# New keys of all eight heads weighed in one passage at a batch's end, with two heads' outputs in each PSUM bank

## What is computed

```python
q = rope(rmsnorm(x @ Wq.T))          # 32 query heads of 128
k = rope(rmsnorm(x @ Wk.T))          # 8 key heads of 128, 32 new keys per sequence
v = x @ Wv.T
k_all = concat([k_cache[block_table], k])    # 512 cached keys, then 32 new ones
v_all = concat([v_cache[block_table], v])
scores = einsum('bqhd,bkhd->bhqk', q, repeat(k_all)) * SCALE      # 4 query heads share a key head
probs = softmax(where(valid, scores, -1e30))
o = einsum('bhqk,bkhd->bqhd', probs, repeat(v_all))
return x + einsum('bse,de->bsd', o.reshape(b, s, 4096), Wo)
```

## Time and profile before

| | us |
|---|---|
| median of 3 runs | 2317.36 |
| lowest and highest | 2316.82, 2319.02 |
| the profiled execution | 2317.06 |
| its span, first to last instruction | 2315.2 |
| TensorE busy in the span | 2260.6 |
| VectorE busy | 1701.7 |
| ScalarE busy | 1296.3 |
| GpSimd busy | 1148.0 |
| attention's weighing, first to last instruction | 732.5 to 1950.3 |

### The profile page before, as it was taken

One profiled execution on the slowest core, in us unless ns is written; L12 is line 12 of the kernel. 1 busy time (PEld: TensorE's weight loads), 2 busy tenths in 40 slices (PEclk: granted clock), 3 DMA queues, 4 the chain that ended last, 5 costly groups with the idle time before them and its releaser, 6 DMA issues. The chain is left out here.

```text
span 2315.2 us, 52251 instructions
## 1 busy us (share of the span) xinstructions
PE 2260.6 (98%) x16384; PEld 1949.7 (84%) x16384; DVE 1701.7 (74%) x3504; ACT 1296.3 (56%) x2643; POOL 1148.0 (50%) x1218
## 2 busy tenths in 40 slices
PE   7998999999998999999999999999999998999999
PEld 6777777777776999999999999999999997888887
DVE  7861788888877888888888888888888886422121
ACT  6733888888875555555555555555555554411110
POOL 5200454544445777777777777777777773000000
PEclk9999999999998999999999999999999999999999
DMA  7543244434448888888888888888888885643442
GB/s 269 204 114 90 85 131 122 132 114 124 132 146 279 287 285 285 287 288 290 291 292 285 291 290 288 295 284 297 286 294 292 287 288 181 206 127 107 129 127 63
DMA packets 451817, 501.70 MB, mean 217 GB/s; under 512 B 95864, under 2 KB 390776, under 8 KB 443417
## 3 DMA queue, kind: packets, MB, share of 16 engines
q1 hardware_dynamic: 414872, 366.44, 48.7%
q0 software_dynamic: 36864, 134.23, 16.2%
HBM read 408.21 MB, written 92.34 MB: 216 GB/s over the span
## 5 line engine op out<-in xcount | busy, mean ns | idle before, releaser
L1296 ACT ACTIVATE att_probs<-att_probs,att_low 128x544 f32<-128x544 f32 x512 | 383.5, 749 | 517.7 <-DVE att_low L1384 452.3
L1192 POOL TENSOR_TENSOR att_probs<-att_probs,att_inverse 128x512 f32<-128x512 f32 x512 | 535.1, 1045 | 273.6 <-DVE att_inverse L1397 269.1
L1253 PE MATMUL att_o<-att_probs_t,att_values 128*128 128x128 f32 x4096 | 541.1, 275 | 1.6 <-DMA att_values<-L_cond_v_cache,att_v_rows_of 1.3
L1384 DVE CUSTOM_DVE_ANT_0 att_probs<-att_score,att_mask,att_batch_cols 128x544 f32<-128x544 f32 x512 | 399.8, 781 | 136.5 <-PE att_score L1218 96.7
L1253 PEld LDWEIGHTS att_o<-att_probs_t,att_values 128*128 128x128 f32 x4096 | 497.6, 192 | 2.0 <-DMA att_values<-L_cond_v_cache,att_v_rows_of 1.5
L1393 DVE COPY att_probs_t<-att_turn 128x512 f32<-128x512 f32 x512 | 351.0, 686 | 1.2 <-PE att_turn L1233 1.2
L1178 POOL DMA_INDIRECT att_values<-L_cond_v_cache,att_v_rows_of x256 | 283.8, 1109 | 82.5 <-POOL att_v_rows_of L1174 50.1
L1233 PE MATMUL att_turn<-ident,att_probs 128*128 128x128 f32 x2048 | 311.2, 274 | 1.2 <-POOL att_probs L1192 0.8
L1005 POOL TENSOR_TENSOR proj_q_out<-proj_by_cos,proj_by_sin 128x512 f32<-128x512 f32 x128 | 188.3, 1471 | 216.3 <-DVE proj_by_sin L931 216.3
L1233 PEld LDWEIGHTS att_turn<-ident,att_probs 128*128 128x128 f32 x2048 | 244.5, 141 | 32.8 <-POOL att_probs L1192 1.4
L862 PE MATMUL proj_proj<-x3t_hi,proj_w_hi 128*128 128x512 f32 x640 | 255.0, 398 | 6.7 <-DVE proj_w_lo L916 6.7
(11 more groups left out here) (156 smaller groups left out, 4151.0 us busy)
## 6 DMA issues: line engine op xcount, KB each, us to landing
keys_first<-L_cond_k_cache SPq DMA_DIRECT2D x512, 128.0 KB
att_keys_raw<-L_cond_k_cache SPq DMA_DIRECT2D x512, 128.0 KB
q_t<-proj_q_out SPq DMA_DIRECT2D x32, 1024.0 KB, 5.3
o_t<-att_heads_out SPq DMA_DIRECT2D x64, 512.0 KB, 6.8
out_o_raw<-o_t SPq DMA_DIRECT2D x31, 1024.0 KB, 5.4
queries_first<-q_t SPq DMA_DIRECT2D x32, 512.0 KB
att_queries_raw<-q_t SPq DMA_DIRECT2D x32, 512.0 KB
maps_even<-L_cond_weight SPq DMA_DIRECT2D x8, 1024.0 KB, 12.0
```

Of the source, the lines that this page charges most:

```text
L1192: nc.gpsimd.tensor_tensor(probs[:, k, 0:L], probs[:, k, 0:L], inverse[:, k:k + 1].to_broadcast([P, L]), ALU.mult).then_inc(probs_ready, 1)
L1253: last = nc.tensor.matmul(o, values[j][:, t, h * D:(h + 1) * D], probs_t[m % 2][:, t * P:(t + 1) * P], start=(t == 0), stop=False, skip_gr ...
L1296: nc.scalar.activation(probs[:, k, :], probs[:, k, :], ACT.Exp, bias=low[k][:, 0:1], scale=-1.0, accum_out=total[k][:, 0:1]).then_inc(exp_ ...
L1384: nc.vector.tensor_tensor_reduce(out=probs[:, k, :], in0=score_ps[:, LEFT:LEFT + KEYS], in1=mask[j][:], scale=batch_cols[j][:, h:h + 1], s ...
```

## The change

After the change there is one passage per batch, after its eighth head. It has eight products (sixteen matmul records in the trace's count) in place of two passages of four. Heads h and h + 4 now share bank h % 4, in columns 0 to 127 and 128 to 255; only heads 0 to 3 start a bank with `start=True`. The eighth head's passage weighs both groups, so both `new_probs_t` tiles are held until then, and TensorE's transposition of a group (`turn`) waits for ScalarE's copy of the group before (`new_kept`). ScalarE's copy of the outputs comes once per batch, in two activations of two banks each, of 512 columns each as before. The weighing of heads 0 and 2 waits for these (`o_ready`) in place of heads 0 and 4. Passages remain in steps 2 and 10 and are gone from steps 6 and 14.

```diff
--- before.py
+++ after.py
@@ -1235,32 +1235,36 @@
                 if m % GH == GH - 1:
                     g = m // GH
 
+                    pe.wait_ge(new_kept, back * (N // GH) + g)
                     pe.wait_ge(group_ready, back * (N // GH) + (g + 1))
                     nc.tensor.transpose(new_ps[:, 0:P], new_group[g % 2].rearrange("p h s -> p (h s)"), ident[:]).then_inc(new_turned, 1)
 
-            def weigh(i, n):
+            def weigh(i, n, first=False):
                 m = n % N
                 back = i if n >= 0 else i - 1
-                j, h, g = m // HK, m % HK, m // GH
+                j, h = m // HK, m % HK
                 if h == 0:
                     pe.wait_ge(v_loaded[j], back * VLD + VLD)
-                if h % GH == 0:
-
-                    pe.wait_ge(o_ready, back * (N // GH) + g)
+                if h % (GH // 2) == 0 and h < GH and (j or not first):
+
+                    pe.wait_ge(o_ready, back * (N // GH) + (j * (HK // GH) - 1 + h // (GH // 2)))
                 pe.wait_ge(kept, i * N + (n + 1))
-                o = o_ps[:, (h % GH) * BANK:(h % GH) * BANK + P]
+                at = (h % GH) * BANK + (h // GH) * P
                 for t in range(PPT):
-                    last = nc.tensor.matmul(o, values[j][:, t, h * D:(h + 1) * D], probs_t[m % 2][:, t * P:(t + 1) * P],
-                                            start=(t == 0), stop=False, skip_group_check=True)
+
+
+                    last = nc.tensor.matmul(o_ps[:, at:at + P], values[j][:, t, h * D:(h + 1) * D], probs_t[m % 2][:, t * P:(t + 1) * P],
+                                            start=(t == 0 and h < GH), stop=False, skip_group_check=True)
                 last.then_inc(weighed[m % 2], 1)
-                if h % GH == GH - 1:
-                    if h == GH - 1:
-                        pe.wait_ge(new_loaded[j], back * NLD + NLD)
-                    pe.wait_ge(new_kept, back * (N // GH) + (g + 1))
-                    for r in range(GH):
-                        rows = slice(r * S, (r + 1) * S)
-                        nc.tensor.matmul(o_ps[:, r * BANK:r * BANK + P], new_values[j][rows, h // GH, :], new_probs_t[g % 2][rows, :],
-                                         start=False, stop=True, skip_group_check=True).then_inc(o_done, 1)
+                if h == HK - 1:
+                    pe.wait_ge(new_loaded[j], back * NLD + NLD)
+                    pe.wait_ge(new_kept, back * (N // GH) + (j + 1) * (HK // GH))
+                    for g in range(HK // GH):
+                        for r in range(GH):
+                            rows = slice(r * S, (r + 1) * S)
+                            at = r * BANK + g * P
+                            nc.tensor.matmul(o_ps[:, at:at + P], new_values[j][rows, g, :], new_probs_t[g][rows, :],
+                                             start=False, stop=True, skip_group_check=True).then_inc(o_done, 1)
 
             def pair(i, first):
                 for n in range(N):
@@ -1268,7 +1272,7 @@
                     if n >= 2 or not first:
                         turn(i, n - 2)
                     if n >= 3 or not first:
-                        weigh(i, n - 3)
+                        weigh(i, n - 3, first)
 
             pair(0, True)
             with pe.Fori(1, PAIRS) as i:
@@ -1302,21 +1306,22 @@
                 back = i if n >= 0 else i - 1
                 g = m // GH
                 act.wait_ge(new_turned, back * (N // GH) + (g + 1))
-                if g or not first:
-
-                    act.wait_ge(o_done, back * N + (g - 1) * GH)
+                if g >= HK // GH or not first:
+
+                    act.wait_ge(o_done, back * N + g // (HK // GH) * HK)
                 nc.scalar.activation(new_probs_t[g % 2][:], new_ps[:, 0:P], ACT.Copy).then_inc(new_kept, 1)
 
             def keep_o(i, n):
 
                 m = n % N
                 back = i if n >= 0 else i - 1
-                j, g = m // HK, m // GH
-                act.wait_ge(o_done, back * N + (g + 1) * GH)
-                if g % 2 == 0:
-                    act.wait_ge(o_stored[j], back * 16)
-                nc.scalar.activation(heads_out[j][:, (g % 2) * GH:(g % 2 + 1) * GH],
-                                     o_ps.rearrange("d (h k) -> d h k", h=GH)[:, :, 0:P], ACT.Copy).then_inc(o_ready, 1)
+                j = m // HK
+                act.wait_ge(o_done, back * N + (j + 1) * HK)
+                act.wait_ge(o_stored[j], back * 16)
+                for r in (slice(0, GH // 2), slice(GH // 2, GH)):
+                    nc.scalar.activation(heads_out[j].rearrange("d (g r) n -> d r g n", r=GH)[:, r],
+                                         o_ps.rearrange("d (r k) -> d r k", r=GH)[:, r, 0:HK // GH * P].rearrange("d r (g n) -> d r g n", n=P),
+                                         ACT.Copy).then_inc(o_ready, 1)
 
             def pair(i, first, last_pair):
                 for n in range(N):
@@ -1341,7 +1346,7 @@
                         nc.scalar.activation(o0_hi[:], o0_raw.rearrange("d b r s -> d r b s"), ACT.Copy).then_inc(o_hi_ready, 1)
                     if n % GH == 1 and (n >= GH or not first):
                         new_part(i, n - 2, first)
-                    if n % GH == 2 and (n >= GH or not first):
+                    if h == 2 and (n >= HK or not first):
                         keep_o(i, n - 3)
 
             split(0, 0, 0, 0)
```

## The result

| | before | after |
|---|---|---|
| median, us | 2317.35 (4 runs) | 2285.8 (4 runs, 2283.72 to 2288.11) |
| the profiled execution and its span, us | 2317.06, 2315.2 | 2286.66, 2284.8 |

A forecast was written before the change was run, and what follows sets the result against it. TensorE was taken as the bound, with GpSimd binding locally in heads 3 to 6 and VectorE at the loop's end. 32 even batches x 0.29 = 9.3 us, odd ones 0, taken as 9: forecast 2308.2 us, range 2305 to 2312.

The forecast's parts named there:

- what a passage costs TensorE: A passage of four costs 0.63 us, the remaining one grows by 0.22; TensorE's own saving 0.41 us a batch.
- GpSimd's chain, even batches: Head 2's product start and the chain after it stay fixed, so steps 7 and 8 wait: gain 0.29 us.
- VectorE's chain, odd batches: Subtractions held by GpSimd's products keep head 7's inverse; mask 0.61 us after the inverse sets step 1: gain 0.
- where TensorE waits for GpSimd: Transpositions of steps 7, 8, 15 and 0 come 0.05 us after a GpSimd product's end; no wait in steps 6, 14.
- the rest costs nothing: ScalarE's second activation of 0.60 us in step 3, the added waits, SyncE's store and load and GpSimd's gather cost nothing.
- The largest gain that I priced: Rival: TensorE's whole saving arrives because GpSimd's chain moves up as well: 2291 us, chance 0.06.
- Both halves gain: Rival: subtractions shorten when started earlier, so odd batches gain 0.29 us too: 18.6 us in all, 2298.5; chance 0.16.
- No change: Rival: the step behind a wait does not speed up (2313 us), or the passage grows by 0.43 (2316); chance 0.18.
- The slower case (single file): Rival: products behind the first four run one after another, passage grows by 0.89 us: 28 us slower, 2345; chance 0.12.
- a longer passage by the increments: Rule against: increments of concurrent tiles serialize at 26.3 ns, adding 0.11 us to the passage's 0.22; some 2310 us.

The follow-up runs named there:

- experiment 2: The changed kernel with four more row-tile products after head 3 of each batch, into columns nobody reads: 2324.58 us, ratio 1.0035 to the kernel before.
- Experiment 5: The changed kernel with two small operations ahead of VectorE's mask building moved behind head 3, so the mask building starts about 0.25 us sooner: 2293.27 us, ratio 0.99.
- Experiment 4: The changed kernel with VectorE's loop turned between steps 2 and 3 in place of steps 15 and 0, instruction order kept: 2284.46 us, ratio 0.9855.
- experiment 8: The changed kernel with VectorE's loop turned behind step 2, and GpSimd's copy of row numbers moved to behind head 1: 2280.96 us, ratio 0.9842.
- experiment 9 with the early copy: On experiment 8's kernel, one passage of sixteen products per pair of batches, four heads' outputs per bank, gathers in heads 3 to 6: 2274.92 us, ratio 0.9825.

## Why the prediction was wrong, and where it was right

**Right: what a passage costs TensorE.** Eight products add 0.65 - 0.43 = 0.22, as forecast. The four products put back in experiment 2 cost 0.61 each passage.

**Wrong: "GpSimd's chain, even batches", the sentence that holds head 2's product fixed and lets the chain "run on" from there.** Its start did stay, and I had checked what could come late, but not whether the durations in it depend on VectorE. The second gather (not among my rows; I had taken a later one, of 1.12, to stand for all) lost 0.20 because VectorE's mask building came 0.22 later. My own sum with this one term changed: step 7's release moves from 1312.92 to 1312.72, before TensorE's 1312.74, so there is no wait and step 8 starts at 1311.97 + 2.09 = 1314.06. Its transposition is released at 1315.26 - 0.20 = 1315.06 and its weighing starts at 1315.44: 0.49 before the 1315.93 of the earlier trace rows, in place of 0.29. Measured: 0.47. Experiment 5 puts the term back and with it the waits in steps 7, 8, 15 and 0. The odd batch has the same shorter gather.

**Wrong: "VectorE's chain, odd batches", the sentence "the next mask starts 0.61 us after the inverse".** The subtractions did what I said. The one ahead of this inverse takes 0.94 us in place of 0.67 and ends at 1321.00, 0.43 after GpSimd's product (1319.51 + 1.06 = 1320.57 in the trace of after). But the 0.61 wasn't a price of its own: it held slack, and in place of the inverse's start it was the exponential of step 15 that set the mask, 0.84 ahead of it, with the turn of the loop between. Experiment 4 moves the turn and the mask moves by 0.25. That exponential follows the scores of step 15, so when TensorE came earlier, the mask did too, and the odd batch gained its 0.49 where the forecast had 0. I saw one distance in one trace and took it for a cause; at that place others were possible.

**Half right: where TensorE waits for GpSimd.** The waits of steps 6 and 14 are gone, as forecast, but for a few odd batches. Step 8's transposition starts 0.05 after GpSimd's product (1302.12 to 1302.17), step 0's 0.12 after (1320.57 to 1320.69; what adds the 0.07 no run tells). Steps 7 and 15 were to wait too and don't: step 7's transposition comes at 0.77 in every pair, step 15's in most (mean 0.795). That is the 0.20 of the gather again.

**Right: the rest costs nothing.** ScalarE's two copies are done before head 0's weighing. Line 1322 on ScalarE in step 3 (answers to the earlier trace rows):

```profile
1290.67 1.09 ACT L1322 ACTIVATE att_heads_out<-att_o 128x512 f32<-128x512 f32 x2 [0.32 <-PE att_o L1266]
1292.62 0.75 ACT L1300 ACTIVATE att_probs<-att_probs,att_low 128x544 f32<-128x544 f32 x1 [0.86 <-DVE att_low L1389]
```

Both end by 1291.76, and the exponential that follows waits for VectorE, as before.

**The rivals.** The largest gain that I priced, 2291 us, was TensorE's 0.41 for each batch. It left out what the wait of step 6 or 14 was worth, though the even batch's sum names it: 0.14 less the 0.05 that the weighing then comes later behind its transposition, 0.09. Together 0.50 x 64 = 32 us, 2285. The result, 2285.8, is close to that, but the rival's reason is not the one: the start of GpSimd's chain did not move up, the chain got shorter, and VectorE's mask moved with TensorE. *Both halves gain* was right in that the odd batch gained, and wrong in its reason, since the subtractions kept their 0.42. Of *No change* neither branch came: behind its wait step 8's weighing follows 0.39 later, and the passage grew by 0.22. The slower case (single file) and a longer passage by the increments didn't come either.

## What to carry to other kernels

Before a chain of another engine is held fixed, look at which of its durations vary from instance to instance, and beside what; here a shift of 0.22 us on a third engine changed a gather by 0.20. A distance between two instructions is a cause only if it stays when something ahead of it moves: over five kernels the 0.61 became anything from 0.20 to 0.76, and the 0.84 stayed. Where one trace can't tell, give both readings a large chance. And price the largest gain with every wait on the path that the change removes, not with the removed work alone, less what the step behind a wait makes up.

## What the runs showed of the hardware

**A gather on GpSimd that starts while VectorE is well into an operation with all its operands in SBUF is held until that operation ends.** Medians over some 200 gathers in the middle of attention in each trace; the recorded length goes by how much of VectorE's operation was left when the gather started:

| VectorE's operation at the gather's start | left, us | the gather takes, us |
|---|---|---|
| copy out of PSUM (L1393, L1398) | 0.18 to 0.40 | 1.00 |
| the small operations ahead of the mask, after | 0.04 | 0.98 |
| subtraction (L1360, L1365) | 0.27 | 1.12 |
| mask building (L1379), experiment 5 | 0.31 | 1.17 |
| mask building (L1371), before | 0.34 | 1.20 |
| subtraction, experiment 8 | 0.35 | 1.21 |
| mask building begun 0.02 before, experiment 9 with the early copy | 0.47 | 0.98 |
| adding the mask to scores in PSUM, experiment 8 | 0.55 | 1.01 |

In the rows with 0.27 to 0.35 left and all operands in SBUF it is one line: 0.86 us plus what was left. The gathers of these rows start 0.13 us or more behind VectorE's operation. The 24 that start only 0.02 behind it are not held, and a mask building that starts 0.07 behind a gather isn't either (0.49 us at 1295.44 in the trace of after, under the gather of 1295.37). The 1.12 of the earlier trace rows, which I had taken for a gather's own length, is a held one too. GpSimd's products hold the subtractions: one that starts up to 0.9 us into a product ends 0.42 us after it, in all 148 such cases in the middle of attention before, and all 153 after. The 45 of experiment 8 that start some 1.0 us into it take their own 0.55 and end 0.51 after. The Trainium skill (SBUF — State Buffer, "Who interferes with whom") says that the two engines share a pair of ports, that whoever issues first gets it for the whole instruction, and that this concerns VectorE's copies and `tensor_scalar` in their fast modes, and operations with two SBUF inputs where GpSimd reads SBUF. The mask building agrees where it started well before the gather, as do the operations that read PSUM, which hold nothing; a mask building held by a gather was not seen. Of operations with two SBUF inputs the Trainium skill infers in the same section that they leave GpSimd's descriptor writing alone; the subtractions in the table hold a gather by the same line as the mask building. What the gather needs of the ports, its row numbers or its descriptors, no run here tells apart.

**Entering and leaving 32-row tiles costs TensorE 0.2 us each.** The weighing before a passage takes 1.10 us up to the first load in place of 0.89, and passages of 8, 16 and 32 load records take 0.43, 0.66 and 1.10 us to the next scores: some 0.2 us plus 0.028 a record. So each of these passages costs 0.4 us besides its products; that the second 0.2 belongs to the leaving is read from the line through three lengths. The Trainium skill (TensorEngine Tiling (Array Packing), "Key Properties") says that a change of tiling mode drains TensorE. The two times 0.2 us agree with it; that they are this drain, no run here shows.

**The turn of VectorE's loop delayed the next mask by 0.25 us** (experiment 4). It runs from the end of the exponential that the loop's last inverse waits for: from there to the mask are 0.84 us, and 0.60 in the mean with the turn elsewhere. An idle time put down to another engine's old signal can hide such a turn: the profile gave it to the scores in the earlier trace rows.
